# Second attention: the probabilities' transpose moved from TensorE to 32x32 blocks on VectorE and SBUF-to-SBUF DMAs, with a longer pipeline of units

## The chip, the core and the metric

The kernel runs on one core of a Trainium2 chip. A core has TensorE (matmuls, with weight loads that overlap them), VectorE, ScalarE, GpSimd, the SP sequencer, which here only issues DMAs, and 16 DMA engines. The metric is the device time of one execution in microseconds, the median of several runs.

## What is computed

Two layers, each a gated cross attention followed by a gated feed-forward, on x of shape 16 batches x 128 tokens x 256, with a context of 16 x 128 x 128. The change touches the attention of the second layer: 16 query heads and 8 key and value heads of width 128, no norm on queries or keys.

```python
q = (text_hidden @ Wq).reshape(B, T_text, N_HEADS, HEAD_DIM).transpose(0, 2, 1, 3)
k = (vision_tokens @ Wk).reshape(B, T_vis, N_KV_HEADS, HEAD_DIM).transpose(0, 2, 1, 3)
...
scores = jnp.einsum('bhtd,bhsd->bhts', q, k) / scale
scores = jnp.where(mask, scores, -jnp.inf)
attn = jax.nn.softmax(scores, axis=-1)
out = jnp.einsum('bhts,bhsd->bhtd', attn, v)
return out @ Wo
```

Behind it stands a mixture of 8 experts, of which each token takes 2, with a shared expert; a router picks them from the normalised result of the attention.

## The kernel before

Everything is in float32. Products that need accuracy are split into a high part (rounded to TensorE's fast 32-bit format, `fp32r`) and a low part (the rest), and made of three matmuls: high x high, high x low, low x high (`three_pass`, lines 98 to 100). Each such product needs a copy on ScalarE for the high part and a subtraction for the low part.

In the second attention the weights are multiplied together first (steps UV, UK, UC, UQ, UO and UM of `SecondWeights`): Wq with Wk, Wv with Wo. So queries meet the raw context and the probabilities multiply the raw context.

The work goes over 4 groups of 4 batches and, in a group, over 4 quads of 4 heads: 64 units of one batch and one quad. Each engine walks through the same list of steps, written out by `second_order`, and runs those that are its own, in that order; semaphores tie the engines together. The steps of a unit:

- Q, Qc: one head's queries of a group's four batches (six matmuls of 512 columns), copied by ScalarE (line 893). One per unit, ahead of it.
- S: scores of four heads (line 791, float32, so each matmul runs twice). Sm: VectorE adds the mask's bias, stores the scores to `probs` and takes the maximum (line 1013), then makes the negated bias from it (line 1022).
- EA, EX: ScalarE's Exp of one and of three heads, with the sum (line 902).
- R: reciprocal of the sums on VectorE (line 1026). Rp: GpSimd scales the probabilities (line 1080).
- T: TensorE transposes the four heads' probabilities into one PSUM bank (line 798). Th: ScalarE copies the high part (line 908). Tl: VectorE subtracts for the low part (line 1029).
- C: probabilities x context (three matmuls of 512 columns). Ch, Cl: ScalarE's and VectorE's split of it (lines 911, 1033).
- W: one head of four batches of the quad before, by the product of Wv and Wo, twelve matmuls of 256 columns, added up in two PSUM banks over the 16 heads. WB does the same by batch in the last quad.
- E: VectorE adds the gated sum to x (line 1048), once a group for two batches each.

Beside these the list places the next group's norm and token transposes (LA, LM, LB, X; line 729), the masked context (CM, CN), and the routing of a finished group (NA to RK, PL and SC; lines 1671, 1678). SC is GpSimd's scatter of rows by indirect DMA, two per step (line 1777). T of unit n stands just ahead of C of unit n: from S to C a unit takes about two slots. SP has almost nothing to do in the attention: it loads each group's context (line 634), the router's weights (lines 1658, 1659) and, after the last Q, the weights of the shared expert and of the experts (lines 1251 to 1255).

Of the kernel before, what the change touches and what calls it, by code (L numbers as in the profile page):

```python
# [207 lines left out]
class SecondWeights:  # L208
# [26 lines left out]
    def place(self, order):  # L235

        self.units = [(name, i) for _, name, i, _ in order if name in self.PER]
        scores = [name for _, name, *_ in order].index("S")
        early = [(name, i) for _, name, i, _ in order[:scores] if name in self.PER]
# [6 lines left out]
        self.early_products = sum(u[0] in self.RELEASED for u in early)  # L246
        self.products = sum(u[0] in self.RELEASED for u in self.units)
# [10 lines left out]
    def made(self, engine, unit):  # L258

        engine.wait_ge(self.products_split if unit[0] in self.RELEASED else self.copied, self.count[unit])  # L260

# [40 lines left out]
    def scalar_step(self, act, name, i):  # L302
# [13 lines left out]
        nc.scalar.activation(target, bank[:, :], ACT.Copy).then_inc(self.copied, 1)  # L316

    def vector_step(self, dve, name, i):
        nc, w = self.nc, self.w
        if name == "MB":  # L320
            dve.wait_ge(self.loaded_m, 32)
            nc.vector.tensor_scalar(w["bias"][:, :], self.maskrow[:, :], 1.0, -MASKED, ALU.subtract, ALU.mult)
# [38 lines left out]

def second_order():

    early = {(0, 0): "LA0", (0, 1): "LA1", (0, 2): "PL0", (0, 3): "E0 E1", (1, 0): "NA0", (1, 1): "NA1", (1, 2): "LB0", (1, 3): "LB1", (2, 0): "LB2",
             (2, 1): "LB3", (2, 2): "X0 X1", (3, 1): "CM0"}
    late = {(0, 0): "RQ1", (0, 1): "RK0 LA2 LA3", (0, 2): "PL1", (0, 3): "SC0", (1, 0): "LM0 SC1", (1, 1): "NA2 NA3 SC2", (1, 2): "NM0 SC3",  # L370
            (1, 3): "NB0 NB1", (2, 0): "NB2 NB3", (2, 1): "NX0 NX1", (2, 3): "RT0 RL0", (3, 1): "RS0", (3, 2): "RQ0", (3, 3): "CN0"}
    early_last = {(0, 2): "PL0", (0, 3): "E0 E1", (1, 0): "NA0", (1, 1): "NA3"}
    late_last = {(0, 0): "RQ1", (0, 1): "RK0", (0, 2): "PL1", (0, 3): "SC0", (1, 0): "NA1 NA2 SC1", (1, 1): "NM0 SC2", (1, 2): "NB0 NB1 SC3",
                 (1, 3): "NB2 NB3", (2, 0): "NX0 NX1", (2, 1): "RT0 RL0", (2, 2): "RS0", (2, 3): "RQ0"}
    final = """
        T0 Th0 Tl0 W0 EX1 S2 R1 Rp1 Sm2 C0 Ch0 Cl0 EA2 RQ1
# [8 lines left out]
    def heads(names, i, k):  # L385

        group, j = divmod(k + i // GB - 1, NQ)
        if k + i // GB < G * NQ:
            order.extend((group, name, i % GB, j + 1) for name in names.split())
# [7 lines left out]
    def beside(words, g, routed):  # L397

        for word in words.split():
# [7 lines left out]
            elif g:  # L407
                order.append((g - 1, name, i, NQ))
# [1932 lines left out]
```

## Time and profile before

| | |
|---|---|
| median of 3 runs | 1318.08 us (1316.62 to 1318.91) |
| profiled execution, span | 1318.3 us |
| mean granted TensorE clock | 0.994 of full |
| TensorE matmuls busy | 1263.8 us, 96% |
| VectorE busy | 897.1 us, 68% |
| ScalarE busy | 773.5 us, 59% |
| GpSimd busy | 429.6 us, 33% |
| DMA through SP's queue | 14.8% of 16 engines' span |
| second attention | about 766 to 1124 us of the span |

Busy times are sums over instructions of an engine. Matmuls are pipelined and the ends of their rows are modelled, so the distance from start to start says what one costs. An engine's idle time is put down to what ended it. Idle time of an engine that does not set the end costs nothing.

### The profile page before, as it was taken

How to read it: one execution, taken by the hardware profiler on the slowest of the kernel's cores; microseconds unless marked ns; L12 is line 12 of the kernel's file. 1: busy time of each engine (PE TensorE's matmuls, PEld its weight loads, DVE VectorE, ACT ScalarE, POOL GpSimd, SP SyncE). 2: the span in 40 equal slices, each digit the busy share in tenths (PEclk: the TensorE clock that was granted, in tenths of full speed). 3: DMA queues.
4: the chain of work that ended last, by engine and by line, in shares of the span. 5: the costliest groups of instructions: out<-in, count | busy, mean ns of one | idle time of the engine just before them, and what ended most of it. 6: DMA issues, size and time to landing. Idle time of an engine off the chain costs nothing. (4 is left out here: it accounts for less than half of the span.)

```text
span 1318.3 us, 23514 instructions
## 1 busy us (share of the span) xinstructions
PE 1263.8 (96%) x8163; PEld 1119.2 (85%) x8163; DVE 897.1 (68%) x2517; ACT 773.5 (59%) x2117; POOL 429.6 (33%) x414
## 2 busy tenths in 40 slices
PE   6899999999999899999999989999999999999998
PEld 4788888888888778888888887999988988888987
DVE  6778788888987676643433355667676676788857
ACT  4777777777777733322222257666666666546642
POOL 3555565555655443100000001222133141222430
PEclk9999999999999989999999989999999999999999
DMA  7000000000000400697000000000000003413435
GB/s 263 9 1 1 9 1 1 9 0 0 0 0 2 102 0 1 187 309 203 41 0 1 0 17 9 1 10 1 1 22 20 1 33 133 117 45 97 122 99 178
DMA packets 62631, 67.54 MB, mean 51 GB/s; under 512 B 14425, under 2 KB 53858, under 8 KB 62146
## 3 DMA queue, kind: packets, MB, share of 16 engines
q1 hardware_dynamic: 59122, 56.89, 14.8%
q0 software_dynamic: 3408, 9.34, 1.9%
q8 instruction: 58, 0.95, 0.3%
q14 instruction: 43, 0.35, 0.1%
HBM read 36.82 MB, written 29.40 MB: 50 GB/s over the span
## 5 line engine op out<-in xcount | busy, mean ns | idle before, releaser
L1080 POOL TENSOR_TENSOR probs_a<-probs_a,rden_a 128x512 f32<-128x512 f32 x128 | 133.1, 1040 | 344.8 <-DVE rden_a L1026 344.0
L98 PE MATMUL bank<-wvo_hi,pc_hi_a 128*128 128x256 f32 x512 | 153.2, 299 | 1.3 <-DVE pc_lo_a L1033 1.3
L1485 ACT ACTIVATE act_g_f<-bank 128x512 f32<-128x512 f32 x64 | 38.2, 597 | 191.2 <-PE bank L100 191.2
L99 PE MATMUL bank<-wvo_lo,pc_hi_a 128*128 128x256 f32 x512 | 143.3, 280 | 0.0
L100 PE MATMUL bank<-wvo_hi,pc_lo_a 128*128 128x256 f32 x512 | 143.2, 280 | 0.0
L1544 DVE TENSOR_TENSOR hid_f<-act_g_f,bank 128x512 f32<-128x512 f32 x64 | 44.0, 687 | 142.5 <-ACT act_g_f L1485 142.5
L911 ACT ACTIVATE pc_hi_a<-bank 128x512 fp32r<-128x512 f32 x128 | 76.6, 599 | 108.2 <-PE bank L100 106.8
L902 ACT ACTIVATE probs_a<-bank,nbias_a,q_r_a 128x128 f32<-128x128 f32 x256 | 114.3, 472 | 23.6 <-DVE nbias_a L1020 23.4
L1029 DVE TENSOR_TENSOR pt_lo_a<-bank,pt_hi_a 128x512 fp32r<-128x512 f32 x128 | 87.8, 686 | 57.4 <-ACT pt_hi_a L908 56.8
L1033 DVE TENSOR_TENSOR pc_lo_a<-bank,pc_hi_a 128x512 fp32r<-128x512 f32 x128 | 88.0, 687 | 43.8 <-ACT pc_hi_a L911 43.7
L902 ACT ACTIVATE probs_a<-probs_a,nbias_a 128x128 f32<-128x128 f32 x256 | 99.8, 397 | 4.7 <-DVE nbias_a L1022 4.4
L98 PE MATMUL bank<-xt_hi_f,w_gu_hi_f 128*128 128x512 f32 (+1 forms) x256 | 101.2, 395 | 0.0
L100 PE MATMUL bank<-xt_hi_f,w_gu_lo_f 128*128 128x512 f32 (+1 forms) x256 | 101.0, 394 | 0.0
L99 PE MATMUL bank<-xt_lo_f,w_gu_hi_f 128*128 128x512 f32 (+1 forms) x256 | 100.4, 392 | 0.0
L98 PEld LDWEIGHTS bank<-wvo_hi,pc_hi_a 128*128 128x128 f32 x512 | 97.1, 190 | 3.0 <-DVE pc_lo_a L1033 2.3
L99 PEld LDWEIGHTS bank<-wvo_lo,pc_hi_a 128*128 128x128 f32 x512 | 97.4, 190 | 0.7
L140 POOL TENSOR_TENSOR rstd<-mv,half 128x4 f32<-128x4 f32 x12 | 12.1, 1012 | 260.4 <-DVE mv L135 260.4
L100 PEld LDWEIGHTS bank<-wvo_hi,pc_lo_a 128*128 128x128 f32 x512 | 96.9, 189 | 0.0
L908 ACT ACTIVATE pt_hi_a<-bank 128x512 fp32r<-128x512 f32 x128 | 76.1, 595 | 24.9 <-PE bank L798 24.7
L798 PEld LDWEIGHTS bank<-ident,probs_a 128*128 128x128 f32 x512 | 62.7, 140 | 22.9 <-POOL probs_a L1080 8.4
L798 PE MATMUL bank<-ident,probs_a 128*128 128x128 f32 x512 | 77.7, 274 | 4.3 <-POOL probs_a L1080 4.3
L98 PE MATMUL bank<-w_down_hi_f,hs_hi_f 128*128 128x256 f32 x256 | 73.1, 285 | 0.7 <-DVE hs_lo_f L1502 0.7
(305 smaller groups left out, 3953.0 us busy)
## 6 DMA issues: line engine op xcount, KB each, us to landing
rows_in<-blank_f SPq DMA_DIRECT2D x8, 2193.0 KB, 21.8
xs_raw_f<-rows_in SPq DMA_DIRECT2D x39, 129.0 KB
y_tok_f<-rows_out SPq DMA_DIRECT2D x4, 1024.0 KB, 9.1
we_raw<-in_L_ffn_We_gate_up SPq DMA_DIRECT2D x2, 1408.0 KB, 10.1
ctx_raw_a<-in_ctx SPq DMA_DIRECT2D x8, 256.0 KB, 2.9
x_sb<-in_x SPq DMA_DIRECT2D x4, 512.0 KB, 10.2
wq_raw<-in_L_xattn_Wq SPq DMA_DIRECT2D x4, 512.0 KB, 7.6
wo_raw<-in_L_xattn_Wo SPq DMA_DIRECT2D x1, 2048.0 KB, 14.0
```

Of the source, the lines that this page charges most:

```text
L98: nc.tensor.matmul(out, w[0], x[0], start=start, stop=False)
L99: nc.tensor.matmul(out, w[0], x[1], start=False, stop=False)
L100: return nc.tensor.matmul(out, w[1], x[0], start=False, stop=stop)
L798: last = nc.tensor.transpose(t_bank[:, h * P:(h + 1) * P], probs[:, i % 2, h, :], core.ident[:, :])
L902: last = nc.scalar.activation(probs[:, i % 2, h, :], s_bank[i % 2][:, h * P:(h + 1) * P] if L == 0 else scores[:, i % 2, h, :], ACT.Exp, b ...
L908: nc.scalar.activation(pt[0][:, :], t_bank[:, :], ACT.Copy).then_inc(sem("pt_hi_ready"), 1)
L911: nc.scalar.activation(flat(pc[0][:, j % 2, i, :, :]), c_bank[:, :], ACT.Copy).then_inc(sem("pc_hi_ready"), 1)
L1029: nc.vector.tensor_tensor(pt[1][:, :], t_bank[:, :], f32(pt[0][:, :]), ALU.subtract).then_inc(sem("pt_ready"), 1)
L1033: nc.vector.tensor_tensor(lo, c_bank[:, :], f32(hi), ALU.subtract).then_inc(sem("pc_ready"), 1)
L1080: nc.gpsimd.tensor_tensor(probs[:, i % 2, :, :], probs[:, i % 2, :, :], scale, ALU.mult).then_inc(sem("probs_scaled"), 1)
L1485: nc.scalar.activation(act_g[:, i % 2, :], g_bank[i % 2][:, :], ACT.Gelu_apprx_tanh).then_inc(sem("gate_read"), 1)
L1544: nc.vector.tensor_tensor(hid[:, i % 2, :], act_g[:, i % 2, :], u_bank[i % 2][:, :], ALU.mult).then_inc(sem("up_read"), 1)
```

## The change

T is gone from TensorE. In its place, for each unit, VectorE transposes the scaled probabilities in 32x32 blocks (step TV, SBUF to SBUF), which puts each block right in itself but leaves it on the wrong partitions. For each pair of units SP then issues 16 DMAs from SBUF to SBUF, one for each pair of partition quarters (32 partitions x 256 columns, 32 KB), from `blocks` to `turned`. Both are double-buffered by pair. Th reads `turned` in place of the PSUM bank; Tl does too and runs on GpSimd in place of VectorE. The PSUM bank that T used is a second bank for C.

The order is written anew, with one unit in each slot v: S and Sm of unit v + 2, EX of v + 1, R and Rp of v, TV of v - 1, Th and Tl of v - 5, C of v - 6, W of v - 7 and Q of v + 7. W is now a unit's own batch with its four heads, in every quad (still twelve matmuls of 256 columns). The loop runs from v = -2 to 71. The eight UO steps stand in slots 0 to 5 where they stood before the first S. `probs` has four buffers in place of two. The scale of the scores, with a negative sign, is in the copy of the key products, so that the maximum becomes a minimum and the negation after Sm goes away. SP's queue holds the pairs' DMAs for the whole attention, the router's weights and the next contexts between them, the shared expert's weights after pair 28 and the experts' after pair 31.

The core of the diff (lines between @@ name the place):

```diff
@@ second_order, new @@
+U = B * NQ
+LAG = 8
...
+    lead = {-2: "UM6 CM0", -1: "UM7 CN0", 0: "UO0", 1: "UO1", 2: "UO2", 3: "UO3 UO4", 4: "UO5 UO6", 5: "UO7"}
+    norm = {0: "LA0", 1: "LA1", 2: "LA2", 3: "LA3", 4: "LM0", 5: "LB0", 6: "LB1", 7: "LB2", 8: "LB3"}
...
+    for v in range(-2, U + LAG):
+        s = v + 2 - LAG
+        if 0 <= v < U - H and v % H == 9:
+            words("X0 X1", v // H + 1)
+        unit(s + 1, "Th", "Tl")
+        unit(v + 2, "S")
+        unit(v, "R", "Rp")
+        unit(v - 1, "TV")
+        unit(v + 1, "EX")
+        unit(s, "C")
+        unit(v + 2, "Sm")
+        words(lead.get(v, ""))
+        unit(s - 1, "W")
+        if 0 <= v < U - H:
+            words(norm.get(v % H, ""), v // H + 1)
+        for r in range(G):
+            table = routing if r < G - 2 else hurried
+            here = table.get(s - r * H, "")
+            words(here if r < G - 1 or here[:1] == "E" else "", r)
+        unit(s, "Ch", "Cl")
+        if 0 <= s < U - H and s % H in (13, 15):
+            words({13: "CM0", 15: "CN0"}[s % H], s // H + 1)
+        words(following.get(s, ""))
+        if s == 4:
+            words("SR0")
+        unit(v + 2, "EA")
+        if v + 7 > 4:
+            unit(v + 7, "Q", "Qc")
...
@@ second_attention, new: buffers @@
+        probs = sb("probs", [P, 4, QH, P])
+        pt = pair("pt", [P, 2, QH * P])
+        pc = pair("pc", [P, 2, QH, P])
+        blocks = sb("blocks", [P, 2, 4, 2, N // 4])
+        turned = sb("turned", [P, 2, 4, 2, N // 4])
...
@@ queue of SP @@
+            prep.load(sp)
+            load(0)
+            for p in range(U // 2):
+                if p == 3:
+                    sp.wait_ge(prep.filled, len(prep.units))
+                    router.load(sp)
+                if p % 8 == 3 and p < 24:
+                    sp.wait_ge(sem("cn_ready"), p // 8 + 1)
+                    load(p // 8 + 1)
+                s = p % 2
+                sp.wait_ge(sem("blocks_made"), 2 * p + 2)
+                if p >= 2:
+                    sp.wait_ge(sem("pt_ready"), 2 * p - 2)
+                for i in range(4):
+                    for j in range(4):
+                        sp.dma_start(turned[32 * j:32 * j + 32, s, i, :, :], blocks[32 * i:32 * i + 32, s, j, :, :]).then_inc(sem(f"turned{s}"), 16)
+                if p == 28:
+                    sp.wait_ge(q_filled, U)
+                    gate_up.load_shared(sp, a)
+            gate_up.load_experts(sp, a)
...
@@ TensorE, C and W @@
+                elif name == "C":
+                    if n % H == 0:
+                        pe.wait_ge(sem("cn_ready"), n // H + 1)
+                    pe.wait_ge(sem("pt_ready"), n + 1)
+                    if n >= 2:
+                        pe.wait_ge(sem("pc_ready"), n - 1)
+                    three_pass(nc, c_bank[n % 2][:, :], [v[:, n % GB, :] for v in cn], [v[:, n % 2, :] for v in pt], True, True).then_inc(sem("c_filled"), 1)
+                elif name == "W":
+                    k, b = divmod(n, GB)
+                    g, j = divmod(k, NQ)
+                    pe.wait_ge(sem("pc_ready"), n + 1)
+                    if n == 0:
+                        pe.wait_ge(prep.products_split, prep.products)
+                    if g and j == 0 and b % 2 == 0:
+                        pe.wait_ge(sem("out_read"), 2 * g - 1 + b // 2)
+                    for h in range(QH):
+                        last = three_pass(nc, out_of(b), [v[:, n % 2, h, :] for v in pc], [v[:, j * QH + h, :] for v in w["vo"]],
+                                          j == 0 and h == 0 and b % 2 == 0, j == NQ - 1 and h == QH - 1 and b % 2 == 1)
+                    last.then_inc(sem("w_done"), 1)
...
@@ ScalarE, Th @@
+                elif name == "Th":
+                    act.wait_ge(sem(f"turned{n // 2 % 2}"), LANDED * (n // 4 + 1))
+                    if n >= 2:
+                        act.wait_ge(sem("c_filled"), n - 1)
+                    nc.scalar.activation(pt[0][:, n % 2, :].rearrange("p (h i t) -> p i h t", h=QH, i=4),
+                                         turned[:, n // 2 % 2, :, n % 2, :].rearrange("p i (h t) -> p i h t", h=QH), ACT.Copy).then_inc(sem("pt_hi_ready"), 1)
...
@@ VectorE, Sm and TV @@
+                elif name == "Sm":
+                    batch = n // H * GB + n % GB
+                    dve.wait_ge(sem("s_filled"), n + 1)
+                    if n >= 4:
+                        dve.wait_ge(sem("blocks_made"), n - 3)
+                    for h in range(QH):
+                        last = nc.vector.tensor_tensor_reduce(probs[:, n % 4, h, :], s_bank[n % 2][:, h * P:(h + 1) * P], w["bias"][:, batch * P:(batch + 1) * P],
+                                                              1.0, 3.0e38, ALU.add, ALU.min, nmin[:, n % 2, h:h + 1])
+                    last.then_inc(sem("min_ready"), 1)
+                elif name == "TV":
+                    p = n // 2
+                    dve.wait_ge(sem("probs_scaled"), n + 1)
+                    if n % 2 == 0 and p >= 2:
+                        dve.wait_ge(*taken(p - 2))
+                    nc.vector.transpose(blocks[:, p % 2, :, n % 2, :].rearrange("p j (h t) -> p h j t", h=QH),
+                                        probs[:, n % 4, :, :].rearrange("p h (j s) -> p h j s", j=4)).then_inc(sem("blocks_made"), 1)
...
@@ GpSimd, Rp and Tl @@
+                elif name == "Rp":
+                    pool.wait_ge(sem("rden_ready"), n + 1)
+                    scale = rden[:, n % 2, :].unsqueeze(2).to_broadcast([P, QH, P])
+                    nc.gpsimd.tensor_tensor(probs[:, n % 4, :, :], probs[:, n % 4, :, :], scale, ALU.mult).then_inc(sem("probs_scaled"), 1)
+                elif name == "Tl":
+                    pool.wait_ge(sem("pt_hi_ready"), n + 1)
+                    hi, lo = (v[:, n % 2, :].rearrange("p (h i t) -> p i h t", h=QH, i=4) for v in pt)
+                    nc.gpsimd.tensor_tensor(lo, turned[:, n // 2 % 2, :, n % 2, :].rearrange("p i (h t) -> p i h t", h=QH), f32(hi),
+                                            ALU.subtract).then_inc(sem("pt_ready"), 1)
...
@@ elsewhere @@
-        nc.scalar.activation(target, bank[:, :], ACT.Copy).then_inc(self.copied, 1)
+        nc.scalar.activation(target, bank[:, :], ACT.Copy, scale=-float(P) ** -0.5 if name == "UK" else 1.0).then_inc(self.copied, 1)
-            nc.vector.tensor_scalar(w["bias"][:, :], self.maskrow[:, :], 1.0, -MASKED, ALU.subtract, ALU.mult)
+            nc.vector.tensor_scalar(w["bias"][:, :], self.maskrow[:, :], 1.0, MASKED, ALU.subtract, ALU.mult)
...
-                    attended = attention(nc, core, block, layer, w, a, gate_up, norm, norm_ffn, packed, router, prep, None)
+                    attended = second_attention(nc, core, block, w, a, gate_up, norm, router, prep)
```

## Rows read from the trace of the kernel before

**Rows 1.** Busy time by stage: span, PE, PEld, DVE, ACT, POOL, clock, DMA.

```profile
795.67:824.00 28.33, 25.98 (x160) 22.31 (x161) 18.68 (x87) 21.69 (x70) 6.24 (x6) 1.00 0.04 10
824.00:1095.40 271.40, 268.23 (x1868) 242.99 (x1867) 183.48 (x793) 178.23 (x604) 78.77 (x85) 1.00 0.03 11
1095.40:1124.20 28.80, 27.21 (x210) 24.70 (x208) 21.69 (x81) 19.62 (x65) 5.20 (x5) 1.00 0.45 151
```

**Rows 2.** The same stretch, line 1033 (Cl, once a unit) alone.

```profile
824.00:1095.40 271.40, 37.10 (x54) 1.00 0.03 11
```

**Rows 3.** Waits of weight loads, 824 to 1095.4: us, times, longest.

```profile
PEld bank L798 <- POOL probs_a L1080: 4.1, 6, 1.2
PEld bank L98 <- ACT tokens_r L1703: 1.6, 3, 0.5
```

**Rows 4.** Timeline of weight loads, one slot: start, duration, first of each step.

```profile
901.79 0.58 PEld L798 LDWEIGHTS bank<-ident,probs_a 128*128 128x128 f32 x4
...
902.34 0.19 PEld L98 LDWEIGHTS bank<-wvo_hi,pc_hi_a 128*128 128x128 f32 x1
...
903.71 0.97 PEld L791 LDWEIGHTS bank<-ctx_t,q_a 128*128 128x128 f32 x8
904.60 0.19 PEld L98 LDWEIGHTS bank<-pt_hi_a,cn_hi_a 128*128 128x128 f32 x1
...
905.18 0.19 PEld L98 LDWEIGHTS bank<-xt_a_hi,wq_hi 128*128 128x128 f32 x1
...
906.55 0.58 PEld L798 LDWEIGHTS bank<-ident,probs_a 128*128 128x128 f32 x4
```

**Rows 5.** Groups by line: busy us, mean ns, idle before.

```profile
L1080 POOL TENSOR_TENSOR probs_a<-probs_a,rden_a 128x512 f32<-128x512 f32 x128 | 133.1, 1040 | 344.8 <-DVE rden_a L1026 344.0 <-issue 0.7
...
L902 ACT ACTIVATE probs_a<-probs_a,nbias_a 128x128 f32<-128x128 f32 x256 | 99.8, 397 | 4.7 <-DVE nbias_a L1022 4.4
...
L1029 DVE TENSOR_TENSOR pt_lo_a<-bank,pt_hi_a 128x512 fp32r<-128x512 f32 x128 | 87.8, 686 | 57.4 <-ACT pt_hi_a L908 56.8
...
L908 ACT ACTIVATE pt_hi_a<-bank 128x512 fp32r<-128x512 f32 x128 | 76.1, 595 | 24.9 <-PE bank L798 24.7
...
L1777 POOL DMA_INDIRECT rows_in<-pay_r,row_of_r x32 | 33.8, 1057 | 28.8 <-DVE pay_r L1774 20.4 <-issue 8.3
...
L1093 POOL TENSOR_TENSOR wk_lo<-wk_raw,wk_hi 128x512 fp32r<-128x512 f32 x2 | 2.6, 1296 | 0.0
```

**Rows 6.** SP's queue, timeline of DMA issues (802.63 follows a one-row load).

```profile
802.27 0.31 SPq L1658 DMA_DIRECT2D raw_r<-in_L_ffn_W_sgate  x1
802.63 0.28 SPq L1659 DMA_DIRECT2D raw_r<-in_L_ffn_W_router  x1
...
1095.40 0.38 SPq L1251 DMA_DIRECT2D ws_raw<-in_L_ffn_Ws_gate_up  x1
1095.83 0.46 SPq L1252 DMA_DIRECT2D ws_raw<-in_L_ffn_Ws_gate_up  x1
1096.34 0.47 SPq L1251 DMA_DIRECT2D ws_raw<-in_L_ffn_Ws_gate_up  x1
```

**Rows 7.** DMA issues of the page: KB each, median us to landing.

```profile
ctx_raw_a<-in_ctx SPq DMA_DIRECT2D x8, 256.0 KB, 2.9
...
out<-x_sb SPq DMA_DIRECT2D x2, 256.0 KB, 2.2
```

**Rows 8.** Waits of weight loads, 1095.4 to 1124.2.

```profile
PEld bank L798 <- POOL probs_a L1080: 1.6, 3, 0.7
PEld bank L98 <- DVE pt_lo_a L1029: 1.0, 2, 0.7
PEld bank L98 <- DVE pc_lo_a L1033: 0.8, 1, 0.8
```

**Rows 9.** The experts' weights: ns min/median/max of their split, first and last start.

```profile
L2132 ACT ACTIVATE we_hi_f<-we_raw x8: 780/784/793, 1138.7 to 1174.3; 128x704 fp32r<-128x704 f32 x8
```

## What I expect and why

> **What bounds the kernel now.** I read the stages first. In the second attention TensorE is the engine that is always at work: in the stretch 824 to 1095.4 us the matmuls are busy for 268.2 of 271.4 us, VectorE for 183.5, ScalarE for 178.2, GpSimd for 78.8 and the DMA engines for 3% [rows 1]. The clock there is granted in full, 2.4 GHz. That stretch holds 54 units (a unit is one batch of one quad of heads) [rows 2], so a unit takes 271.4/54 = 5.03 us. Next I read the waits of TensorE in it: in 271 us the weight loads waited 4.1 us for GpSimd's scaled probabilities at the transposes and 1.6 us for ScalarE [rows 3]. It is work, not waiting, that fills the stretch, so a matmul that is taken out shortens it. Then the start times of the weight loads in one slot [rows 4]: transposes 901.79 to 902.34 (0.55 us), W to 903.71 (1.37), S to 904.60 (0.89), C to 905.18 (0.58; the first transfer from S to C overlaps), Q to 906.55 (1.37). A plain slot is 4.76 us; the 0.27 us up to 5.03 are the routing, token transposes and waits, spread over all units.
>
> **What is removed.** 64 units x 4 PE transposes: 64 x 0.55 = **35.2 us** of the bounding engine, and with them the waits on their input, 4.1 us. VectorE loses the 64 small negations after Sm (the sign moves into the key products) and the subtraction Tl, which goes to GpSimd. All of that was hidden, so it is worth nothing by itself. The plain slot becomes 4.21 us, the mean one 5.03 - 0.55 = 4.48.
>
> **What is added, engine by engine, against 4.48 us.**
> VectorE: each of the 64 units gets one transpose of 128x512 in blocks. No row shows a block transpose. The nearest are the 128x512 elementwise operations, 0.69 us [rows 5]; below that it can't go far, since these read every column once too, and as upper bound I take twice that, 1.37. At 0.69 it takes the place of the moved Tl, which cost the same, so VectorE stays at 183.5/54 = 3.4 us per unit; at 1.37 it is 4.1, still under 4.48, with stalls where routing bunches up (I give those up to 5 us). I take 0.69.
> ScalarE: the same four Exp (0.40 us each) and three 128x512 copies (0.60) [rows 5], 178.2/54 = 3.3 us per unit. Th now reads SBUF; same size, taken equal.
> GpSimd: Rp at 1.04 as before and Tl new. The nearest row is its own subtraction of 128x512, 1.30 us [rows 5]. With 78.8/54 = 1.46 before, that is 2.8 us per unit. In the slots with SC it also issues two indirect DMAs at 1.06 each [rows 5]: 1.04 + 1.30 + 2.12 = 4.5 us in four slots in a row, a little over the plain slot. It falls some 1 to 2 us behind, and TensorE needs its product only in the next slot. All of these new frictions together I price at 2 us (0 to 8).
>
> **The queue of SP, the new resource.** For each pair of units SP issues 16 DMAs of 32 partitions x 1 KB. What counts is the pace of issue. Issues back to back, each with 128 or more partition rows, start 0.43 and 0.51 us apart; one with a single row is followed 0.36 us later [rows 6]. These 32-row DMAs lie between: I take 0.40, bounds 0.30 and 0.55. A pair then costs SP 6.4 us (4.8 to 8.8) against a period of two slots, 8.4 us plain and 8.96 mean. So the throughput fits, up to 8.96/16 = 0.56 us per DMA.
> Latency: the pair's second TV and the Tl that frees its half of `turned` both run in slot 2p+2, the latter about 2.8 us into it (Th late by the previous Qc, 0.8; Th 0.6; Tl 1.3). The data are due when ScalarE comes to Th three slots later, 12.6 + 0.8 us: 10.6 us for 6.4 + landing. Landings of a store and of a load of 256 KB are 2.2 and 2.9 us [rows 7]; 6.4 + 2.5 = 8.9, so it is hidden with 1.7 us to spare. TV of the unit that refills the pair's `blocks` waits for the same landing, in slot 2p+5 too; there VectorE would stand, with Sm and Cl behind it. If that cover is gone ScalarE stands at Th, and behind it stand EX, Ch, EA and Qc of that slot, and for Ch and Qc waits TensorE; but C needs the product a further slot later, so the first 2 us or so still cost nothing. The loads of the router's weights and of the next context now stand between the pairs in SP's queue (five DMAs in the whole stage, at pairs 3, 11 and 19, 0.4 to 0.5 us each); what they wait for is long done by then, and a pair's slack of 2 us takes them. Bytes are no issue: 512 KB per pair in 8.96 us is 58 GB/s, against the 151 GB/s that the end stretch shows [rows 1].
> The Trainium skill, DMA: Bandwidth & Descriptors, section Rules for kernel authors, speaks against this change: small transfers should be joined, since under 64 KB one pays mostly overhead. These are 32 KB. The same page gives a fixed cost of about 2 us for one DMA; by the rows the issues are 0.5 us apart whatever they take to land, so the overhead overlaps and only the pace counts. If it did not overlap, that is rival 3 below.
>
> **The start.** Eight UO units move from before the first S into the first eight slots; same work, and the slots need something to fill them, as C and W start only at v = 6. A lead slot has S + Q + UO, about 3.1 us. From TV of unit 1 (v = 2, about 1 us in) to Th of unit 0 (v = 5) there are 3 x 3.1 - 1 = 8.3 us for 6.4 + 2.5 = 8.9. Cost about 1 us more than now (0 to 4).
>
> **The end.** This is where the longer pipeline shows. After the last Q (slot 56) a slot has 0.89 + 0.69 + 1.37 = 2.95 us of TensorE up to slot 61, then C + W = 2.06. Counting from slot 57 TensorE needs 5 x 2.95 + 8 x 2.06 + 1.37 = 32.6 us. SP: pair 28 may start at slot 58 + 2 = 5.0 and is issued by 11.4. Then the four loads of the shared weights, 4 x 0.5 = 2.0, to 13.4. Pairs 29, 30, 31 follow without a gap, 3 x 6.4: 32.6. Last landing 34.4. Then Th 0.6, two Tl 2.6, C 0.7, Ch and Cl with their hand-overs 1.5, W 1.4: 41.2. So 8.6 us of waiting (6 at 0.30, 15 at 0.55); what TensorE waits in the same place now is 3.4 us of weight-load waits [rows 8]. Net **+5.2**. The expert weights are issued after pair 31, 8 us before the attention ends instead of 27. The first one used is read 14 us after the end [rows 9], so this is covered.
>
> **Sum.** -35.2 (transposes) - 4.1 (their waits) + 2 (frictions) + 1 (start) + 5.2 (end) = -31.1 us. The profiled execution has a span of 1318.3 us, 0.2 from the median of the three runs, 1318.08; so the sum is made against the median without a correction: 1287 us. The later feed-forward is left as it is; its TensorE work is unchanged. Since the unpriced things (semaphore hops, 16 completions on one count) can only add, I put 1 us on top: **1288**.
>
> **Rivals.**
> Rival 1, the queue paces the pairs in part: DMAs at 0.50 to 0.58 us. By the sum of the end this is +13 instead of +5, the latency cover of 10.6 us is overrun in every pair (8 + 2.5 and more), and some 5 to 15 us of the steady gain go: 1297 to 1312. For it: the 0.51 of rows 6. Against: those carry four times as many rows or more. The same range covers a block transpose of twice 0.69 us, or a GpSimd Tl that is slower on its rearranged columns.
> Rival 2, slower than before: SP sets the whole stage. The first pair starts about 803 us, 512 DMAs x t, then 4.5 us for other loads and 9 us of tail: end at 816 + 512 t. That is later than today's 1124.2 from t = 0.60 us on; at 0.70 it is 1174, so 1318 + 50 = 1368; at 0.62 it is 1328. For it: issue times in bursts grow in the profile when the queue is loaded. Against: all short issues in rows 6 are below 0.52.
> Rival 3: each DMA waits for the one before to land: 16 x 2.2 = 35 us per pair, 32 pairs, 1126 us for the stage: 2100 us. The spacing in rows 6 speaks against it; the loads there land after several us each and start 0.5 apart.
> Rival 4: less than the price. With t at 0.30 and GpSimd and VectorE never late, -35.2 - 4.1 + 2.6 = -36.7: 1281.
>
> **Chances.** Forecast (1281 to 1296) 0.63; rival 4 or below 1281, 0.06; rival 1 (1297 to 1314) 0.18; rival 2 0.10; rival 3 0.01; the 0.02 left lie about no change. A difference of 0.2%, 2.6 us, is about what a measurement of this kernel can tell from none. Faster: 0.63 + 0.06 + 0.18 = 0.87; same 0.02; slower 0.11. The range 1279 to 1310 leaves out rivals 2 and 3, the top of 1 and the bottom of 4, near 2 in 10 together.
>
> **What would show it.** Right: in the stretch of the attention no LDWEIGHTS from probabilities, slots 4.21 us apart, VectorE's transpose near 0.69 and GpSimd's Tl near 1.3 us, SP's issues 0.4 us apart with a pause between pairs, and TensorE idle only in the last 30 us, for DVE's or POOL's products that hang on a DMA. Rival 1: pauses of SP vanish and ScalarE waits for `turned`. Rival 2: TensorE idle in every second slot. A block transpose above 2 us, or a landing above 5 us, would make the prediction wrong in the same way.

## The result, and the profile after

The changed kernel takes 1352.15 us (median of 4 runs, 1347.03 to 1353.26) against 1317.51 us for the kernel before, run beside it: a ratio of 1.0254, interval 1.0235 to 1.0273. The forecast was 1288 us, range 1279 to 1310. It was wrong, and in sign: +34 us in place of -30.

I begin with the chain that ended last. This is section 4 of the page of the changed kernel; before, SP's queue had no part in the attention to speak of.

```profile
span 1350.4 us, 23692 instructions
PE 1259.5 (93%) x7907; PEld 1111.3 (82%) x7907; DVE 894.4 (66%) x2453; ACT 770.6 (57%) x2117; POOL 510.1 (38%) x478
## 4 chain that ended last, share of the span: by engine, by line
SPq 22%; PE 13%; DVE 3%; issue 2%; ACT 1%; POOL 0%; DMA 0%; DVEq 0%
```

22% of the span, some 300 us, is SP issuing DMAs. Next the issues themselves, line 1176, which answer to [rows 6], and the waits of SP, VectorE, ScalarE and TensorE in the attention, which answer to [rows 3] (engine, line, what it waited for: us in total, times, longest):

```profile
L1176 SPq DMA_DIRECT2D turned_a<-blocks_a x512: 507/591/1879, 802.4 to 1143.8; - x171
```
```profile
SPq L1176 <- DVE blocks_a L1333: 34.3, 3, 33.4
...
DVE blocks_a L1333 <- DMA turned_a<-blocks_a: 80.7, 28, 6.4
...
ACT pt_hi_a L1280 <- DMA turned_a<-blocks_a: 82.5, 27, 7.0
...
PEld bank L98 <- POOL pt_lo_a L1368: 30.7, 14, 4.3
PEld bank L98 <- DVE pc_lo_a L1338: 17.8, 20, 2.8
```

Of SP's 34.3 us of waiting, 33.4 are the wait for the first pair. After it SP waits 0.9 us in all: 512 DMAs between 802.4 and 1143.8 us, (1143.8 - 802.4)/512 = 0.667 us each, all other loads included. One issue lasts 0.59 us (median). A pair of units needs 16 x 0.667 = 10.7 us of SP, and a pair of TensorE's slots is under 9. So the queue falls behind, and VectorE and ScalarE stand at `turned` in nearly every pair (28 and 27 times in 32), as rival 2 said.

The stage windows answer to [rows 1] (stretch, its length, busy us and count of each engine, granted clock, DMA share, GB/s):

```profile
766.00:800.00 34.00, 34.00 (x225) 31.73 (x224) 16.95 (x61) 25.50 (x61) 2.74 (x3) 0.92 0.09 17
800.00:824.00 24.00, 23.98 (x140) 20.95 (x138) 16.40 (x78) 17.22 (x60) 9.09 (x9) 1.00 0.16 44
824.00:1100.00 276.00, 247.68 (x1578) 219.15 (x1578) 169.91 (x702) 169.87 (x586) 136.96 (x130) 0.97 0.21 58
1100.00:1158.80 58.80, 41.40 (x217) 36.34 (x216) 34.33 (x96) 24.34 (x68) 23.52 (x21) 0.77 0.41 126
```

The start is full. From 824 to 1100 TensorE stands for 28.3 us, and in the last 58.8 us for 17.4 more, at a granted clock of 0.77. The last matmul of the attention starts at 1158.5 us; before, it was 1123.9. That difference, 34.6 us, is the whole result. How the end looks in TensorE's weight loads (start, duration, in brackets the wait and its cause):

```profile
1142.85 0.19 PEld L100 LDWEIGHTS bank<-wvo_hi,pc_lo_a 128*128 128x128 f32 x1
1142.98 0.46 PEld L1525 LDWEIGHTS bank<-ident,pay_r 128*128 128x128 f32 x4
1147.78 0.29 PEld L98 LDWEIGHTS bank<-pt_hi_a,cn_hi_a 128*128 128x128 f32 x1 [4.34 <-POOL pt_lo_a L1368]
...
1155.84 0.33 PEld L98 LDWEIGHTS bank<-wvo_hi,pc_hi_a 128*128 128x128 f32 x1
1156.06 0.33 PEld L99 LDWEIGHTS bank<-wvo_lo,pc_hi_a 128*128 128x128 f32 x1
```

TensorE waits 4.34 us for the last pair, and after it the weight loads of W start 0.21 us apart where they start 0.11 to 0.12 apart at full clock. The engine that stood has come back at the 1.2 GHz level: the clock granted from 1147.7 to 1157.1 us is 0.50. That holds for all that is left but the last unit's W, whose loads from 1157.28 on are 0.11 to 0.12 us apart again.

The operations of VectorE, ScalarE and GpSimd, from section 5 of the page (count, busy us, mean ns, idle before and its cause), answer to [rows 5]:

```profile
L1368 POOL TENSOR_TENSOR pt_lo_a<-turned_a,pt_hi_a 128x512 fp32r<-128x512 f32 x64 | 82.4, 1287 | 162.3 <-ACT pt_hi_a L1280 162.2
L1333 DVE STREAM_TRANSPOSE blocks_a<-probs_a 128x512 f32<-128x512 f32 x64 | 44.8, 700 | 81.7 <-DMA turned_a<-blocks_a 81.7
L1280 ACT ACTIVATE pt_hi_a<-turned_a 128x512 fp32r<-128x512 f32 x64 | 40.1, 626 | 83.6 <-DMA turned_a<-blocks_a 83.6
```

These three are as forecast: 0.70 us for the block transpose (0.69 forecast), 1.29 for Tl (1.30), 0.63 for Th (0.60).

### The profile page after: what moved, and what is told of

Same layout as the page of the kernel before. It is cut to its first block and busy times, and to the rows that moved or that the text cites. A ratio compares the mean times of both kernels' runs of the same rounds, so it can differ in the third digit from the quotient of the medians.

```text
span 1350.4 us, 23692 instructions
## 1 busy us (share of the span) xinstructions
PE 1259.5 (93%) x7907; PEld 1111.3 (82%) x7907; DVE 894.4 (66%) x2453; ACT 770.6 (57%) x2117; POOL 510.1 (38%) x478
## 5 line engine op out<-in xcount | busy, mean ns | idle before, releaser
L100 PE MATMUL bank<-wvo_hi,pc_lo_a 128*128 128x256 f32 x512 | 147.9, 289 | 0.0
L99 PE MATMUL bank<-wvo_lo,pc_hi_a 128*128 128x256 f32 x512 | 147.8, 289 | 0.0
L1368 POOL TENSOR_TENSOR pt_lo_a<-turned_a,pt_hi_a 128x512 fp32r<-128x512 f32 x64 | 82.4, 1287 | 162.3 <-ACT pt_hi_a L1280 162.2
L99 PEld LDWEIGHTS bank<-wvo_lo,pc_hi_a 128*128 128x128 f32 x512 | 101.7, 199 | 2.6
L100 PEld LDWEIGHTS bank<-wvo_hi,pc_lo_a 128*128 128x128 f32 x512 | 101.4, 198 | 0.0
L1272 ACT ACTIVATE probs_a<-probs_a,nmin_a 128x128 f32<-128x128 f32 x256 | 99.5, 391 | 3.3 <-DVE nmin_a L1322 3.2
L1333 DVE STREAM_TRANSPOSE blocks_a<-probs_a 128x512 f32<-128x512 f32 x64 | 44.8, 700 | 81.7 <-DMA turned_a<-blocks_a 81.7
L98 PE MATMUL bank<-pt_hi_a,cn_hi_a 128*128 128x512 f32 x128 | 61.2, 478 | 36.7 <-POOL pt_lo_a L1368 27.9
L1280 ACT ACTIVATE pt_hi_a<-turned_a 128x512 fp32r<-128x512 f32 x64 | 40.1, 626 | 83.6 <-DMA turned_a<-blocks_a 83.6
L1075 POOL TENSOR_TENSOR q_r_a<-q_ss_a,half 128x4 f32<-128x4 f32 x64 | 63.4, 1012 | 26.5 <-DVE q_ss_a L977 26.5
```

Source lines behind the costliest of these rows:

```text
L98: nc.tensor.matmul(out, w[0], x[0], start=start, stop=False)
L99: nc.tensor.matmul(out, w[0], x[1], start=False, stop=False)
L100: return nc.tensor.matmul(out, w[1], x[0], start=False, stop=stop)
L1075: nc.gpsimd.tensor_tensor(q_r[:, (j + 1) % 2, i, :], q_ss[:, i, :], core.half[:, 0:QH], ALU.pow).then_inc(sem("q_norm_ready"), 1)
L1272: last = nc.scalar.activation(probs[:, n % 4, h, :], probs[:, n % 4, h, :], ACT.Exp, bias=nmin[:, n % 2, h:h + 1], scale=-1.0, accum_out=d ...
L1333: nc.vector.transpose(blocks[:, p % 2, :, n % 2, :].rearrange("p j (h t) -> p h j t", h=QH), probs[:, n % 4, :, :].rearrange("p h (j s) -> ...
```

## What an issue costs, and on what it depends

All experiments edit the changed kernel, except where said. The medians of the kernel before, run beside the experiments, were 1317.2 to 1318.5 us.

**Without the DMAs.** This asks whether SP's queue is the whole cause.

```diff
-                for i in range(4):
-                    for j in range(4):
-                        sp.dma_start(turned[32 * j:32 * j + 32, s, i, :, :], blocks[...])
@@ Th, Tl @@
-    turned[:, n // 2 % 2, :, n % 2, :]
+    blocks[:, n // 2 % 3, :, n % 2, :]
```

> Leaves out all 512 SBUF-to-SBUF DMAs (ScalarE and GpSimd read VectorE's blocks where they are, so the product uses unswapped probabilities); order, block transposes, Th and Tl are those of the changed kernel. Theory A, SP's pace of issue alone makes the changed kernel slow: the stage is TensorE-bound again, slots 4.21 us, 1318 - 35.2 - 4.1 + 2 + 1 plus an end of about 3 = 1285 us (1279 to 1292). Theory B, the new order or the engines (Tl on GpSimd, TV on VectorE) also hold it back: above 1300. Theory C, a slower clock comes with the new code whatever it waits for: TensorE granted under 0.98 here too.

Measured: 1306.99 us (1304.58 to 1307.40), ratio to the kernel before 0.9915 (0.9899 to 0.9932). `blocks` has three buffers in this run, since Th and Tl read it themselves; the runs below that keep two buffers and a queue that keeps up take the same time (1304.6 to 1305.6 us). The queue costs 1352 - 1307 = 45 us, which makes it the cause of the sign. But 1307 is not 1285, so theory B holds beside A: some 20 us of the forecast are lost elsewhere. They are taken up further down.

The windows of this run, beside those above, say where the 45 us lie:

```profile
766.00:800.00 34.00, 33.07 (x226) 30.76 (x227) 17.42 (x61) 25.17 (x62) 2.81 (x3) 0.95 0.10 17
800.00:824.00 24.00, 24.00 (x142) 21.20 (x141) 21.01 (x91) 20.83 (x72) 11.28 (x11) 1.00 0.04 12
824.00:1055.00 231.00, 227.36 (x1514) 205.41 (x1513) 167.96 (x671) 161.90 (x558) 127.45 (x121) 0.99 0.03 8
1055.00:1113.90 58.90, 45.44 (x278) 40.03 (x277) 42.40 (x118) 29.01 (x87) 31.52 (x28) 0.88 0.28 93
```

The attention is 392.8 us long with the queue and 347.9 without, 44.9 apart. TensorE stands for 45.7 us in the one and 18.0 in the other, which makes 27.7. The other 17.2 us are the same matmuls taking longer (347.1 us busy against 329.9), at granted clocks of 0.97 and 0.77 in the last two stretches against 0.99 and 0.88. Waiting shows as waiting only in part; the rest of it shows as slower work.

**A quarter of each row.** From pair 2 on each DMA moves 32 partitions x 256 B in place of 1 KB.

```diff
-    sp.dma_start(turned[32 * j:32 * j + 32, s, i, :, :], blocks[32 * i:32 * i + 32, s, j, :, :])
+    sp.dma_start(turned[32 * j:32 * j + 32, s, i, 0, 0:64], blocks[32 * i:32 * i + 32, s, j, 0, 0:64])
```

> From the third pair on each of the 16 DMAs moves 64 of the 256 columns (256 B in place of 1 KB a row), same number of DMAs and rows; the rest of each row keeps older data. Theory A (a fixed cost for each issue): SP's issues still 0.63 us apart, time 1350 within 5. Theory D (the transfers themselves hold the queue back): the pace falls towards 0.3 us and the time towards 1290.

Measured: 1349.69 us (a single run); the issues last 507/591/1645 ns (least, median, longest), to the nanosecond the median of the full rows. The bytes don't set the price.

**Twice the rows, half the DMAs.** 8 DMAs of 64 partitions per pair.

```diff
-                    for j in range(4):
-                        sp.dma_start(turned[32 * j:32 * j + 32, s, i, :, :], blocks[32 * i:32 * i + 32, s, j, :, :])
+                    for j in range(2):
+                        sp.dma_start(turned[64 * j:64 * j + 64, s, i, :, :], blocks[64 * (i // 2):64 * (i // 2) + 64, s, 2 * j + i % 2, :, :])
```

> 8 DMAs of 64 partitions in place of 16 of 32 for each pair: the same bytes and the same number of rows, half the issues (a swap of halves, not the right transpose). Theory A, if the cost is per issue: 8 x 0.63 = 5.1 us a pair against 8.96, TensorE-bound, 1288 to 1296. If the cost of an issue is by its rows (0.02 us a row): 1.26 us apart and 1350 as before.

Measured: 1304.56 us (a single run), as without any DMA. The 1288 to 1296 expected of theory A missed by 9 us, since it rests on the 1285 expected above for a kernel without the DMAs; the 1350 of the rival is far off. The issue keeps its price with twice the partitions, and SP now pauses 30 times for `turned` to be free:

```profile
L1176 SPq DMA_DIRECT2D turned_a<-blocks_a x256: 461/597/1936, 801.3 to 1095.9; - x128
```
```profile
SPq L1173 <- POOL pt_lo_a L1368: 121.5, 30, 7.3
```

**Twelve of the sixteen.** From pair 2 on the four DMAs of the diagonal are left out.

```diff
+                        if i != j or p < 2:
```

> Leaves out the 4 DMAs of each pair whose source and target partitions are the same (from the third pair on; those blocks keep older data): 12 issues in place of 16. Theory A: 12 x 0.64 + one long issue of about 1 us = 8.3 to 8.7 us a pair against a TensorE period of 8.96, so the steady part is just covered and only the end waits, about 13 us: 1292 to 1304. If the pace is set by something else than the number of issues: 1340 to 1350.

Measured: 1310.13 us (a single run), issues again 591 ns, and 0.633 us from start to start in most cases. Twelve nearly fit: 12 x 0.633 = 7.6 us per pair, and ScalarE waits for `turned` 5 times in place of 27. This too is above the range expected (1292 to 1304), for the same reason as the run with eight. Between 12 and 16 lies the edge from which the queue sets the time.

So an issue has a price of its own, whatever it moves. But why 0.63 us from start to start, of which the issue itself is 0.59, where [rows 6] have 0.43 and 0.51? Those were loads from HBM.

**From HBM in place of SBUF.** Same number, same destinations, same waits; only the source is another.

```diff
-    sp.dma_start(turned[32 * j:32 * j + 32, s, i, :, :], blocks[32 * i:32 * i + 32, s, j, :, :])
+    sp.dma_start(turned[32 * j:32 * j + 32, s, i, :, :], a["x"][p % B, 32 * i:32 * i + 32, :].rearrange("s (u c) -> s u c", u=2))
```

> Leaves out the transposed probabilities: each pair's 16 DMAs of 32 partitions x 1 KB read rows of x in HBM in place of `blocks`, so the attention's output is of other numbers, with the same number of issues, the same destinations and the same waits. Theory A (the price is of one issue, whatever it moves and from where): issues 0.63 us apart, last W near 1158 us, about 1350 us. Rival B (the price is of reading and writing SBUF in one transfer): issues 0.43 to 0.51 us apart as for the loads of the kernel before, SP's queue no longer sets the pace, 1305 to 1312 us.

**From SBUF to HBM.** The other end is in HBM.

```diff
@@ on top of the run without the DMAs @@
+                for i in range(4):
+                    for j in range(4 if p < 29 else 0):
+                        sp.dma_start(swap[p % 3, i, j], blocks[32 * i:32 * i + 32, p % 3, j, :, :])
```

> Leaves the moves between the partitions out of the transpose (Th and Tl read `blocks`, as in the run without DMAs), but SP issues for pairs 0 to 28 the 16 DMAs of 32 partitions x 1 KB from `blocks` to HBM. Theory A (an issue costs 0.59 us only where both ends are SBUF): 0.34 to 0.45 us each. Rival B (reading SBUF costs it): 0.59 us. Nothing waits closely for these stores, so the time is 1305 to 1310 us by both.

Measured: 1305.47 and 1304.52 us, a single run each. The issues of line 1176 of the first and 1175 of the second:

```profile
L1176 SPq DMA_DIRECT2D turned_a<-in_x x512: 310/421/1650, 802.8 to 1099.9; - x171
```
```profile
L1175 SPq DMA_DIRECT2D swap<-blocks_a x464: 302/421/1881, 800.6 to 1064.4; - x155
```

Both have a median of 0.42 us, against 0.59 with both ends in SBUF, and most start 0.46 us apart against 0.63, so that sixteen per pair fit: rival B of the first holds, theory A of the second. The difference of 0.17 us is there only where source and destination are both in SBUF; neither reading nor writing SBUF costs it alone. Why that is so stays open; what is shown is the price.

**Four of sixteen on ScalarE's queue.**

```diff
+                        if j < 3 or p == 0:
                             sp.dma_start(turned[32 * j:32 * j + 32, s, i, :, :], ...)
@@ ScalarE, behind Th of an even unit, p = n // 2 + 1 @@
+                        for i in range(4):
+                            act.dma_start(turned[96:128, p % 2, i, :, :], blocks[32 * i:32 * i + 32, p % 2, 3, :, :])
```

> The whole computation. Of each pair's 16 DMAs SP issues 12 and ScalarE's own queue 4, behind its Th of an even unit. Theory A (the 0.63 us is time of SP's own sequencer): SP needs 12 x 0.63 = 7.6 us per pair and keeps up as in the run with twelve; ScalarE has 4 x 0.6 = 2.4 us more per pair, 3.3 + 1.2 = 4.5 us per unit, about the slot: 1312 to 1325 us. Rival B (both queues share one generator of descriptors, which needs 0.6 us per DMA): 16 x 0.63 = 10 us per pair as before, and ScalarE's issues wait for SP's: 1345 to 1365 us.

Measured: 1312.17 us (a single run), with the full computation. Each queue pays its own price:

```profile
L1177 SPq DMA_DIRECT2D turned_a<-blocks_a x388: 507/591/2069, 803.1 to 1105.1; - x194
```
```profile
L1289 ACTq DMA_DIRECT2D turned_a<-blocks_a x124: 514/614/869, 815.0 to 1100.3; - x124
```

The 0.59 us is time of the issuing sequencer, and a second sequencer runs beside it. The Trainium skill, DMA: Bandwidth & Descriptors, section Rules for kernel authors, says that spreading DMAs over several engines brings no bandwidth and "only saves sequencer issue time"; this run agrees on the issue time, which was nearly all that the queue cost here: 40 of the 45 us come back. On bandwidth it says nothing.

**Through HBM, five issues per pair.** If only the number of issues and the pair of ends count, then one store of all of `blocks` and four loads should do.

```diff
+                sp.dma_start(swap[s].rearrange("i c j u n -> (i c) j u n"), blocks[:, s, :, :, :])
+                sp.wait_ge(sem(f"stored{s}"), 16 * (p // 2 + 1))
+                for j in range(4):
+                    sp.dma_start(turned[32 * j:32 * j + 32, s, :, :, :], swap[s, :, :, j, :, :].rearrange("i c u n -> c i u n"))
```

> The whole computation. In place of 16 SBUF-to-SBUF DMAs per pair, one store of `blocks` (512 KB) to HBM and four loads of 32 partitions each: 5 issues in place of 16. Theory A (only the number of issues costs): 5 x 0.6 = 3 us of SP per pair, the two landings of 2 to 3 us fit the 10.6 us of cover, last W near 1112 us, 1303 to 1309 us. Rival B (the bytes or the two landings cost too: 1 MB per pair of 8.7 us, 120 GB/s, and 3 + 3 + 3 + 3 us of latency against 10.6): waits of ScalarE for `turned` in every pair, 1315 to 1345 us.

Measured: 1305.61 us (1303.73 to 1307.79), ratio 0.9910 (0.9888 to 0.9931), with the full computation, as fast as without any move. The store's issue lasts 0.34 us, the loads' 0.43; the landings from section 6 of its page:

```profile
swap<-blocks_a SPq DMA_DIRECT2D x32, 512.0 KB, 2.6
turned_a<-swap SPq DMA_DIRECT2D x128, 128.0 KB, 2.9
```

Twice the bytes (1 MB per pair) and two landings in a row cost nothing: 2.6 + 1.7 + 2.9 us fit the 10.6 us of cover that the prediction worked out.

## The other 20 us: the transposes' price, and the end

**The transposes issued twice.** This edits the kernel before and measures the first term of the sum alone.

```diff
-                    for h in range(QH):
+                    for h in [*range(QH)] * (2 if L == 1 else 1):
                         last = nc.tensor.transpose(t_bank[:, h * P:(h + 1) * P], probs[:, i % 2, h, :], core.ident[:, :])
```

> The kernel before with each unit's four TensorE transposes issued twice into the same bank, 64 x 4 more. Theory A (the price read from the start times, 0.55 us per unit, holds a part of the matmul ahead; four transposes cost 0.42 to 0.44): +27 to +28 us, 1344 to 1347. Rival B (0.55 is their price): +35 us, 1353 us.

Measured: 1344.62 us (1344.07 to 1345.54) against 1318.45, ratio 1.0205 (1.0184 to 1.0226). That is +26.2 us, 0.41 us per unit, not 0.55. (In its trace TensorE is busy in the attention for 27.5 us more, 377.8 against 350.2, and stands for 1.5 less, so up to 0.43 per unit is work.) Its trace shows eight of them in 1.00 us, the next step's first row ending the count:

```profile
931.24 0.19 PEld L100 LDWEIGHTS bank<-xt_a_hi,wq_lo 128*128 128x128 f32 x1
931.46 1.02 PEld L798 LDWEIGHTS bank<-ident,probs_a 128*128 128x128 f32 x8
932.46 0.19 PEld L98 LDWEIGHTS bank<-wvo_hi,pc_hi_a 128*128 128x128 f32 x1
```

Four take 0.55 us and eight take 1.00. The 0.55 I read in [rows 4] was the distance between two weight loads, and it holds a tail of the 512-column matmul ahead. That tail is paid whatever comes next, as the run without the DMAs shows, where W stands right behind C, a step of 512 columns:

```profile
905.40 0.19 PEld L98 LDWEIGHTS bank<-wvo_hi,pc_hi_a 128*128 128x128 f32 x1
905.63 0.19 PEld L99 LDWEIGHTS bank<-wvo_lo,pc_hi_a 128*128 128x128 f32 x1
905.75 0.19 PEld L100 LDWEIGHTS bank<-wvo_hi,pc_lo_a 128*128 128x128 f32 x1
```

The first distance is 0.23 us, the next 0.12; in [rows 4], with T ahead of W, T's 0.55 us held that extra 0.11. Without T the slot shrinks from 4.76 to 4.34 us, as the starts of S in the run without the DMAs show (903.82 and 908.16): 0.42, not 0.55. Eight or nine us of the forecast were never there.

**The end.** In the run without the DMAs TensorE stands for 13.5 of its last 58.9 us, at a granted clock of 0.88 (windows above); before, it stood for 1.6 of the last 28.8, at 1.00. GpSimd's timeline of that run shows why (start, duration, in brackets the idle time before):

```profile
1059.65 1.28 POOL L1363 TENSOR_TENSOR pt_lo_a<-blocks_a,pt_hi_a 128x512 fp32r<-128x512 f32 x1
1060.88 1.04 POOL L1359 TENSOR_TENSOR probs_a<-probs_a,rden_a 128x512 f32<-128x512 f32 x1
1062.08 1.01 POOL L2030 DMA_INDIRECT rows_in<-pay_r,row_of_r  x1 [0.16 <-issue]
1063.40 0.96 POOL L2030 DMA_INDIRECT rows_in<-pay_r,row_of_r  x1 [0.30 <-issue]
1064.38 1.28 POOL L1363 TENSOR_TENSOR pt_lo_a<-blocks_a,pt_hi_a 128x512 fp32r<-128x512 f32 x1
```

A round of Tl, Rp and two scatters takes 4.73 us, and GpSimd never rests. With Q's 1.27 us in it, TensorE's slot is 4.34 and hides nearly all of that; behind the last Q (slot 56) the slot is 3 us. The four scatter steps of group 1 stand in just these slots, and TensorE's matmuls wait 0.56, 1.50 and 0.90 us for Tl in three slots in a row. But waits for Tl are only 3.5 of the 13.5 us; the other 10.0 are for Cl, some in the same slots and some after them. How many of those come from GpSimd's delay the waits don't tell, so two runs take its load away in different ways.

**The scatters three units earlier.** On top of the run without the DMAs.

```diff
-            table = routing if r < G - 2 else hurried
+            table = routing if r < G - 3 else {**hurried, 32: "SC0", 33: "SC1", 34: "SC2", 35: "SC3"} if r < G - 2 else hurried
```

> No DMAs between the partitions, as in the run without them (part of the transpose is left out), and the scatters of group 1 stand three units earlier, so that they lie before the last Q and not in the short slots behind it. Theory A (the 17 us that TensorE stands in the last 60 us come from GpSimd, which has Rp 1.05, Tl 1.29 and two indirect DMAs of 1.06 per slot there, 4.5 us against slots of 3): waits in the last stretch fall below 10 us, 1296 to 1302 us against 1307. Rival B (the short slots stall in themselves, by the chain C, Ch, Cl, W): 1305 to 1308 us.

Measured: 1296.70 us (1294.43 to 1299.01), ratio 0.9838 (0.9818 to 0.9857), 10 us less. Theory A holds in the time, but not in the waits that it named: those of the weight loads in the last stretch fell only from 17.5 to 13.3 us, not below 10. From 766 us on TensorE stands for 5.7 us less, 4.1 of them behind 1055 us, and its matmuls take 3 us less. Nor does this run single out the scatters. The `hurried` table in the edit moves the rest of group 1's routing up by one to three units as well, and VectorE is busy for 16.0 us between 1055 and 1080 in place of 21.3. The next run leaves the order alone.

**Tl on VectorE.** On top of the same run, with the scatters where they were.

```diff
@@ GpSimd's branch for Tl goes, VectorE gets it @@
+                    nc.vector.tensor_tensor(lo, blocks[:, n // 2 % 3, :, n % 2, :].rearrange(...), f32(hi), ALU.subtract)
```

> As the run without DMAs (Th and the low part read `blocks`, so the moves are left out of the transpose), but Tl is VectorE's again. Theory A (GpSimd's load, Rp 1.05 + Tl 1.29 + scatters, is what TensorE's waits at the end come from): GpSimd falls to 1.5 us per unit, VectorE rises to 4.1 of 4.34, waits at the end below 10 us, 1297 to 1303 us. Rival B (VectorE at 4.1 of 4.34 us becomes late in the slots with norm and routing): 1307 to 1316 us.

Measured: 1296.43 us (1294.51 to 1297.57), ratio 0.9837 (0.9816 to 0.9859). Again 10 us less, though VectorE carries 0.7 us more per unit. Rival B falls. The time is as theory A has it, even 0.6 us under its range, but the weight loads still wait 13.2 us at the end and not less than 10. Here the order is as it was and VectorE has more to do, so the gain is GpSimd's: Tl on GpSimd, which I had taken as nearly free, was one part of a collision. TensorE stands for 8.3 us in the last stretch in place of 13.5, all of it for Cl, so a good half of the standing at the end stays when GpSimd's load is gone.

## A version that is faster than both

**Through HBM, with the earlier scatters.** The two repairs together.

> The whole computation: the block transposes through HBM with 5 issues per pair, and the scatters of group 1 three units earlier. Theory A (the two repairs are independent, 47 us for the queue and 10 us for the scatters): 1352 - 47 - 10 = 1295, range 1292 to 1300 us, faster than the kernel before by 1.5% or more. Rival B (the earlier scatters collide with the moves through HBM): 1302 to 1308 us.

Measured: 1297.11 us (1293.56 to 1299.76, 5 runs), ratio 0.9843 (0.9819 to 0.9867), with the full computation: 21 us faster than the kernel before and 55 faster than the changed one. Its last stretches:

```profile
824.00:1055.00 231.00, 227.99 (x1528) 205.63 (x1527) 169.19 (x676) 163.58 (x562) 133.03 (x126) 1.00 0.39 125
1055.00:1103.60 48.60, 40.16 (x275) 35.00 (x275) 34.94 (x112) 28.57 (x83) 25.84 (x23) 0.96 0.61 196
```

The end is 48.6 us long in place of 58.9, at a granted clock of 0.96 in place of 0.88. DMA is at 61% there without harm.

**Do the two repairs of the end add up?** Once with both, once with Tl on VectorE alone.

> The whole computation: the moves through HBM (5 issues per pair), the scatters of group 1 three units earlier, and Tl on VectorE. Theory A (both late repairs take the same load off GpSimd at the end, so they don't add): 1293 to 1298 us, as with one of them. Rival B (what is left of the waits at the end is GpSimd's still): 1286 to 1291 us, near the forecast of the change. Rival C (VectorE, at 4.1 of 4.34 us with the waits for its buffers, is late now): 1300 to 1308 us.

> The whole computation: the moves through HBM and Tl on VectorE, the scatters where the change has them. Theory A (as without the moves, Tl on VectorE takes off 10 us of GpSimd's load at the end): 1294 to 1298 us. Rival B (VectorE has to wait for the stores through HBM before it refills `blocks`, with more work behind it than before): 1300 to 1308 us.

Measured: 1296.19 us (1295.86 to 1298.12), ratio 0.9839 (0.9826 to 0.9852), with both; 1298.86 us (1296.85 to 1300.62), ratio 0.9847 (0.9832 to 0.9863), with Tl alone, which lies between the ranges of its theory and its rival. The three intervals overlap, and a second gain of 10 us would be 1287: the repairs take away the same thing, once. GpSimd is busy for 10.8 of the last 47.5 us with both, and nothing is left there to gain from it; TensorE still stands for 8.5 us in that stretch:

```profile
1055.00:1102.50 47.50, 38.95 (x279) 33.84 (x278) 38.95 (x134) 28.61 (x85) 10.78 (x10) 1.00 0.63 200
```

VectorE is now the busiest engine beside it (38.95 us), and the waits are for its Cl. Whether they come from its load or from the hand-overs C, Ch, Cl, W in short slots was not tried.

## Why the prediction was wrong, step by step

- **The queue of SP** (0.40 us per DMA, 0.30 to 0.55): this failed, and it decided the sign. Measured 0.59 us per issue and 0.667 from one to the next over the stage. I had bounded it by the number of partition rows, between a DMA of one row and DMAs of 128. The runs show that neither rows (64 partitions: 0.60) nor bytes (a quarter: 0.59) matter, while something I had not looked at does: both ends in SBUF. None of the issues of [rows 6] had that. The bound of 0.55 was a little above the top of the nearest rows (0.51) and not that of the unknown; the prediction sets these DMAs apart from the rows by their size and never by their two ends.
- **Throughput limit of 0.56 us per DMA**: near. With the measured price of the transposes the mean slot is 5.03 - 0.41 = 4.62 us and the limit 2 x 4.62/16 = 0.58. Most HBM-sided DMAs start 0.46 us apart and fit; the SBUF-to-SBUF ones at 0.63 don't.
- **Rival 2, end at 816 + 512 t**: right in mechanism and formula. With t = 0.667 it gives 1157.5; the attention's last matmul starts at 1158.5. Its price was 1318 + 33 = 1351 us; measured 1352. It had a chance of 0.10. The argument against it, that all short issues in [rows 6] are below 0.52, was of loads from HBM. Rival 1 had the right mechanism too, but its 0.50 to 0.58 us ended just below the measured price.
- **The transposes**, -35.2: mis-sized; the doubling gives 26.2. A distance between starts is a step's price only where the step ahead leaves no tail.
- **Their waits**, -4.1: gone, but replaced. TensorE stands for 3.6 us between 824 and 1055 without the DMAs, before for 3.2 between 824 and 1095.4. The gain of 4 and the friction of 2 came to nothing together.
- **VectorE's transpose, Th, Tl**: right to 0.03 us in duration.
- **Frictions** of GpSimd and **the end**, +5.2 for the queue: these two failed together. I worked out that GpSimd needs 4.5 us in a slot with scatters (4.73 measured) and compared it with the plain slot. I also worked out that slots behind the last Q are 2.95 us. I did not put the two side by side and ask which slots hold the scatters. The price is 10 us, by two repairs; 8 to 9 us of standing at the end stay with either, mostly in waits for VectorE's Cl, and the sum had such waits only behind the last unit. SP's tail, for which I had put the 5.2, does not exist once the queue keeps up; with the scatters in place TensorE stands for 12 us more in the last stretch than before (13.5 against 1.6), and its matmuls take 6 us longer than the removed 26.2 us leave room for (329.9 us busy from 766 on, against 350.2 - 26.2 = 324.0), for which the lower granted clock is enough: by my estimate from the windows, length times the clock not granted, 11 us are lost by it without the DMAs and 3 before (these at 0.90, from 766 to 795.67).
- **The start**, +1: a small gain. TensorE stands for 0.9 us between 766 and 824 without the DMAs (0.0 with them, 0.6 to 2.8 in the runs through HBM), before for 3.2.
- **The latency cover**, 10.6 us: holds, as two landings in a row through HBM show.
- **The Trainium skill**, DMA: Bandwidth & Descriptors, section Rules for kernel authors: I weighed its rule that small transfers should be joined and set it aside, since issues overlap their landings. They do, but joining pays all the same, by the issues it saves: 8 in place of 16, or 5 through HBM, each bring back about 47 us.

With the terms as measured: 1318 - 26 (transposes) + 0 (their waits and the frictions) - 2 (start) + 12 (standing at the end) + 6 (clock) = 1308, beside 1307 without the DMAs; 45 for the queue make 1353, beside 1352. The 12 and the 6 are read from the run that they explain, and the 45 is the difference of the two times, so only the 26 is a test from outside.

## What to carry to other kernels

Price a DMA issue by a row of the same kind, source and destination memory included, and where none exists let the range run past the point from which the queue decides; a queue that needs 16 issues per period has an edge that one tenth of a microsecond crosses. Cut the number of issues first where the queue's pace sets the time, even by a detour of twice the bytes. And lay each engine's busiest slot beside the shortest slot of the bounding engine, not beside the mean one, since a pipeline's drain has the shortest slots.

## What the runs showed of the hardware

- One DMA issue on SP lasts 0.59 us with both ends in SBUF (32 partitions x 256 B or 1 KB; 0.60 with 64 partitions), 0.42 us with one end in HBM, either one (32 partitions x 1 KB), and 0.34 us for a store of 128 partitions. On ScalarE's queue the first kind lasts 0.61 us, beside SP's.
- Single issues last up to 1.9 us; with these, and the few other loads, the 0.63 us that stand between most starts become 0.667 on average. With one end in HBM most starts are 0.46 us apart.
- VectorE's transpose of 128x512 float32 in 32x32 blocks takes 0.70 us, as its elementwise operations of this size.
- A TensorE that stood 4.3 us came back at half clock and stayed there for 9.4 us of work; the clock granted behind 1055 us was 0.88 in the run without the DMAs and 0.90 to 1.00 in the five with GpSimd relieved.
